# A four-layer transformer on one core: layer three's attention scores as full-array matmuls, and layer four's shared expert taken out of its attention

## The chip, the cores and the metric

One core of one Trainium2 chip runs the whole model in one launch. The metric is the device time in microseconds (us); lower is better. The kernel before takes 2572.56 us, the median of 3 runs (2572.2 to 2572.8).

## The reference

`x` is 16 sequences of 256 tokens, 128 wide, float32. Each of the four layers (0 to 3 in the code; "layer 2" below is the third, "layer 3" the fourth) computes `x + attention(LN(x)) + ffn(LN(x))`. What the change touches:

```python
# layer 2, attention: 16 heads of 8, causal
logits = einsum('bhsd,bhtd->bhst', q, k) / sqrt(8); masked; softmax; @ v; @ w_out
# layer 3, attention: 16 heads of 8, plus a 32-wide rotary part that all heads share
scores = einsum('bqhd,bkhd->bhqk', q, k) + einsum('bqr,bkr->bqk', q_rope, k_rope)[:, None]
scores = scores / sqrt(8 + 32); masked; softmax; @ v; @ W_o
# layer 3, ffn: 8 experts, each token to its best 2, and a shared expert for every token
out    = sum over the 2 chosen e: gate * (gelu(xf @ w1[e] + b1[e]) @ w2[e] + b2[e])
shared = gelu(xf @ ws1 + bs1) @ ws2 + bs2        # 128 -> 512 -> 128
return out + shared
```

## The kernel before

Tokens stand in 8 chunks of 512 (two sequences each). Every layer 1 to 3 runs five stages in this order, each closed for all engines before the next begins: R (normalise, turn, router logits), T (routing on VectorE, one step), A (attention), M (experts, on 256-slot tiles), C (combine: add the gated expert results to `x`). PE, ScalarE (ACT), VectorE (DVE), GpSimd (POOL) and SyncE (SP, which issues most DMAs) each have their own program in this order, tied by semaphores. `STAGES` (L76) gives each stage its count of steps, and `event(...)` (L395 on) how many times per step a semaphore is raised.

**Attention of layers 2 and 3** (`attention`, L951 for ACT, L1317 for PE, L2014 for DVE). A chunk has 16 steps; a step is one pair of heads of one sequence. In step p PE does, in this order: `scores(p)` (keys x queries, with minus the row maximum in an extra row, then the causal mask added by a 128-row matmul with the identity), `turn_maxima`, `average(p-1)` (18 matmuls of 9 columns), `maxima(p+LEAD)` (queries x keys, only to find the row maxima; again with masks), then `turn_o`, `out_proj` and a piece of the next chunk's projections (`prepare`). ACT reads each of the two score banks twice with Exp (`exps`, L1013). POOL makes the low half of the probabilities (`pair_low`, L763) and then, while any are left, sends one tile of 128 token rows to the experts' slots (`send_row_tile`, L744). DVE reduces the maxima (L2120, L2121). SP moves q and k rows through DRAM into stacks (`put_rows`, `load_heads`) and the maxima into the stacks' extra row (`send_rows`).

**The two layers' stacks.** In layer 2 a head stands on 32 rows of the stack: `rows_of` (L1387) returns rows 32j to 32j+32, so a score matmul contracts over 32 rows, and the two heads of a step lie on two different strips of the array. In layer 3 `rows_of` returns all 128 rows (96 rotary, 24 of the head's own, the maximum's row and blanks).

**The shared expert** is inside layer 3's attention: after `exps` of steps 9 to 12 ACT computes one quarter (128 of 512 hidden units) with Gelu (`shared`, L1022); PE computes the quarter's up product in the same steps (`shared_up`, L1478) and its down product one step later (`shared_down`, L1484), in float32; DVE adds the sum to `x` at step 14. Exp and Gelu are in different function tables.

**The router of layer 3** turns a chunk (4 transposes) and multiplies it by the router's weights (4 small matmuls) per chunk; the last combination (C3) has no work of PE or ACT. The outputs are sent after the last combination loads are issued (L709 to L711).

Of the kernel before, what the change touches and what calls it, by code (L numbers as in the profile page):

```python
# [22 lines left out]
ALU = mybir.AluOpType  # L23
ACT = mybir.ActivationFunctionType
# [6 lines left out]
P = 128  # L31
# [44 lines left out]
STAGES = {"N0": NCH, "L0": NCH}  # L76
# [66 lines left out]
def build_program(nc, A, out):  # L143
    ctx = ExitStack()
    with ctx:
# [21 lines left out]
        head_rows = nc.dram_tensor("head_rows", [2, HEADS, 4, 8, CHUNK], HALF).ap()  # L167
# [118 lines left out]
        shared_h = probT  # L286
        cT3 = oT[:, 1, :]
        q_stack = qT[:, 0:2, :].rearrange("p a c -> p (a c)").bitcast(HALF).rearrange("p (g c) -> p g c", g=4)
# [18 lines left out]
        def stack4(a):  # L307
# [5 lines left out]
        head_q = [stack4(far_stacks[:, 0:2048]), stack4(far_stacks[:, 4096:6144]), stack4(near_stacks[:, 0:2048]),  # L313
                  stack4(kT[:, :, :].rearrange("p a c -> p (a c)").bitcast(HALF))]
        head_k = [stack4(far_stacks[:, 2048:4096]), stack4(far_stacks[:, 6144:8192]), stack4(near_stacks[:, 2048:4096]),
                  stack4(region[:, 3072:4096].bitcast(HALF))]
# [10 lines left out]
        sco = [duo[:, 0, :], duo[:, 1, :]]  # L327

# [20 lines left out]
        blank_put = sem("blank_put")  # L349
# [45 lines left out]
        sh_up = event("sh_up", A3=FB)  # L395
        sh_act = event("sh_act", A3=FB)
        sh_down = event("sh_down", A3=FB)
        sh_added = event("sh_added", A3=1)
# [17 lines left out]
        c_step = event("c_step", C1=1, C3=1)  # L416

# [52 lines left out]
        HEAD0 = 96  # L470

# [49 lines left out]
        def _(sp):  # L521
# [53 lines left out]
            def feed_attention(layer):  # L575
# [7 lines left out]
                if layer == 2:  # L583
                    sp.wait_ge(stack_set, 1)
                    for kind in range(2):
                        sp.dma_start(head_rows[kind][:, 0, kind:8, :],
                                     k_stack[0:(8 - kind) * HEADS, 0, :]).then_inc(blank_put, 16)
                    sp.dma_start(head_rows[1][:, 0, 0, :], q_stack[0:HEADS, 0, :]).then_inc(blank_put, 16)
                    sp.wait_ge(blank_put, 48)

                def put_rows(n, kind):
# [5 lines left out]
                    for b, plane in enumerate(planes[kind]):  # L597
                        sp.dma_start(head_rows[kind][:, b + 1, :, :], parts[:, plane, :]).then_inc(rows_put[kind], 16)

                def load_heads(n, g, kind):  # L600
# [3 lines left out]
                    if layer == 3:  # L604
                        proj_read_v.wait(sp, stage, n, rope_made[kind])
                        sp.dma_start((head_q, head_k)[kind][g][0:HEAD0, :, :],
# [4 lines left out]
                    if layer == 2:  # L611
                        sp.dma_start((q_stack, k_stack)[kind][:, g, :], own.rearrange("j b e c -> (j b e) c"))\
                            .then_inc(stack_in[g], 16)
                    else:
                        sp.dma_start((head_q, head_k)[kind][g][HEAD0:P, :, :], own.rearrange("j b e c -> (b e) j c"))\
                            .then_inc(stack_in[g], 16)

                def send_rows(i, e):
# [4 lines left out]
                    dst = q_stack[0:P:GROUP, g, own] if layer == 2 else head_q[g][HEAD0:HEAD0 + 1, :, own]  # L623
                    sp.dma_start(dst, nm_rows[:, b, :]).then_inc(nm_in[b], 16)
# [192 lines left out]
        def _(act):  # L817
# [49 lines left out]

            def router(layer):
# [8 lines left out]
                with act.Fori(0, NCH - 1) as i:  # L877
                    turned_chunk(i + 1, False)
# [94 lines left out]
            def attention(layer):  # L973
# [48 lines left out]
                def shared(i, n):  # L1022
                    sh_up.wait(act, stage, i, n)
                    if n >= 2:
                        sh_down.wait(act, stage, i, n - 2)
# [1350 lines left out]
```

## Time and profile before

| | |
|---|---|
| median of 3 runs | 2572.56 us |
| the profiled execution's own time | 2563.02 us |
| its span (first to last instruction) | 2561.1 us |
| mean granted TensorE clock | 0.82 |
| PE busy, ACT busy, DVE busy, POOL busy | 1926.5, 1300.0, 1557.2, 1140.6 us |

Times of rows count from the span's start. PE is the matmul, PEld the weight load. "PEclk" is the granted TensorE clock, 1.00 being the higher of its two levels (2.4 GHz) and 0.50 the lower (1.2 GHz). A float32 matmul shows as two instructions. Layer 2's attention lies at about 1172 to 1616 us, layer 3's router and routing at 1776 to 1819, its attention at 1819 to 2345, its experts up to 2527, the last combination from there to the end.

### The profile page before, as it was taken

Reading aid. Unit: us, or ns where it says so; the run is one execution under the profiler, and the core shown is the slowest. Engines: PE = TensorE matmul, PEld = TensorE weight load, DVE = VectorE, ACT = ScalarE, POOL = GpSimd, SP = SyncE. Lnnn points to the kernel's source line nnn. Section 1 sums busy time; section 2 is a strip of 40 time slices with the busy share of each in tenths; the row PEclk is TensorE's granted clock in tenths of the full one; section 3 lists DMA queues with packets and bytes.
Section 4 is the critical chain, followed back from the end, with each engine's and each line's share of the span. In section 5 each row is a group of like instructions: output and inputs, shape, how many; then the busy total and the mean of one; then the engine's idle time right before and its main releaser. Section 6 shows DMA issues by size and latency. Waiting matters only on the chain.

```text
span 2561.1 us, 61860 instructions
## 1 busy us (share of the span) xinstructions
PE 1926.5 (75%) x21198; PEld 1285.9 (50%) x21199; DVE 1557.2 (61%) x3642; ACT 1300.0 (51%) x2667; POOL 1140.6 (45%) x921
## 2 busy tenths in 40 slices
PE   1553899899999688625999999682478877876993
PEld 0223566666666566522444444462255555554662
DVE  2236788787888788764444444576555555553775
ACT  0231577676777555302555555550166666665552
POOL 0003577674555233311764455342066664442552
PEclk9785899999999999955555565795689889997997
DMA  8900000020000111211211112121243333330224
GB/s 225 171 2 0 12 18 17 18 78 4 2 2 2 37 45 46 73 41 47 59 43 34 34 43 84 30 58 41 59 108 97 97 94 79 84 83 12 63 63 125
DMA packets 168827, 142.85 MB, mean 56 GB/s; under 512 B 16408, under 2 KB 155000, under 8 KB 168608
## 3 DMA queue, kind: packets, MB, share of 16 engines
q1 hardware_dynamic: 154944, 111.69, 17.9%
q0 software_dynamic: 11584, 23.91, 2.8%
q10 hardware_dynamic: 2080, 4.19, 0.5%
q8 instruction: 153, 2.51, 0.4%
q14 instruction: 66, 0.54, 0.1%
HBM read 62.04 MB, written 52.28 MB: 45 GB/s over the span
## 4 chain that ended last, share of the span: by engine, by line
PE 44%; DVE 19%; issue 12%; ACT 11%; POOL 9%; DMA 2%; DVEq 1%; SPq 1%; ACTq 0%; POOLq 0%
PE duo L1150 11%; PE mo L1150 8%; PE misc L1150 7%; PE ob L1150 7%; POOL v L765 6%; PE acc L1150 6%; ACT v L1020 3%; PE pt L1150 3%; ACT v L1019 2%; DVE nmax L2234 2%; DVE v L1933 2%; ACT L1019 2%; DVE region L2237 1%; ACT L1026 1%; DVE x L2003 1%
## 5 line engine op out<-in xcount | busy, mean ns | idle before, releaser
L765 POOL TENSOR_TENSOR v<-v 128x768 f16<-128x768 f32 x256 | 420.2, 1642 | 519.0 <-ACT v L1020 517.5
L760 POOL TENSOR_TENSOR v<-v 128x512 f16<-128x512 f32 x256 | 290.5, 1153 | 259.9 <-DVE region L2237 259.7
L787 POOL DMA_INDIRECT results<-probT,dest_no x202 | 218.2, 1080 | 325.4 <-ACT probT L819 285.2
L1150 PE MATMUL ob<-wm,v 128*128 128x9 f16 (+1 forms) x5856 | 258.2, 180 | 116.1 <-POOL v L765 94.6
L1150 PEld LDWEIGHTS ob<-wm,v 128*128 128x128 f16 x5856 | 216.7, 100 | 202.3 <-issue 95.0
L2120 DVE TENSOR_REDUCE nm<-duo 128x2 f16<-128x256 f32 x256 | 108.8, 425 | 332.1 <-PE duo L1150 332.1
L1019 ACT ACTIVATE v<-mo 128x384 f32<-128x384 f32 x352 | 174.2, 495 | 192.8 <-PE mo L1150 188.4
L1091 ACT ACTIVATE v<-mo 128x512 f32<-128x512 f32 x256 | 153.4, 599 | 161.1 <-PE mo L1150 161.1
L2234 DVE TENSOR_REDUCE nmax<-duo 128x2 f32<-128x512 f32 x256 | 164.9, 686 | 85.8 <-PE duo L1150 85.8
L1150 PE MATMUL duo<-kT,wm 128*128 128x256 f16 x1212 | 171.8, 279 | 54.7 <-DVE kT L1921 29.2
L1020 ACT ACTIVATE v<-mo 128x384 f16<-128x384 f32 x352 | 175.5, 499 | 0.0
L2121 DVE TENSOR_REDUCE nm<-duo 128x2 f16<-128x512 f32 x256 | 174.3, 681 | 0.0
L746 POOL DMA_INDIRECT slot_rows<-xd,slot_no x160 | 160.5, 1003 | 26.0 <-issue 25.7
L1150 PE MATMUL mo<-qT,kT 64*128 64x256 f16 (+2 forms) x1888 | 169.2, 286 | 0.0
L933 ACT ACTIVATE v<-duo,cols 128x256 f32<-128x256 f32 x248 | 104.1, 471 | 104.6 <-PE duo L1150 99.1
L1150 PEld LDWEIGHTS duo<-kT,wm 128*128 x1212 | 112.5, 99 | 81.3 <-issue 66.5
L1092 ACT ACTIVATE v<-mo 128x512 f16<-128x512 f32 x256 | 153.1, 598 | 0.0
L1925 DVE TENSOR_TENSOR v<-v 128x512 f16<-128x512 f32 x202 | 139.2, 689 | 4.4 <-ACT v L819 0.2
L1200 PE MATMUL pt<-ident,tmp 128*128 128x128 f32 x96 | 26.4, 431 | 143.7 <-DVE tmp L1777 139.1
L1150 PEld LDWEIGHTS mo<-qT,kT 64*128 64x128 f16 (+1 forms) x1888 | 81.3, 97 | 99.0 <-issue 87.8
L1150 PE MATMUL duo<-mask,ident 128*128 128x256 bf16 x512 | 130.4, 348 | 0.0
L1019 ACT ACTIVATE v<-pt 128x384 f32<-128x384 f32 x160 | 79.3, 496 | 84.2 <-PE pt L1150 82.3
(286 smaller groups left out, 4300.0 us busy)
## 6 DMA issues: line engine op xcount, KB each, us to landing
prob<-slot_rows SPq DMA_DIRECT2D x101, 130.0 KB, 2.2
head_rows<-v SPq DMA_DIRECT2D x96, 128.0 KB
load<-wm SPq DMA_DIRECT2D x32, 384.0 KB, 3.7
qT<-results SPq DMA_DIRECT2D x40, 256.0 KB, 3.1
qT<-head_rows SPq DMA_DIRECT2D x48, 128.0 KB, 2.1
qT<-wm SPq DMA_DIRECT2D x16, 384.0 KB
slot_rows<-prob SPq DMA_DIRECT2D x4, 1300.0 KB, 22.0
kT<-head_rows SPq DMA_DIRECT2D x40, 128.0 KB, 2.5
```

The costliest lines, as they stand in the source:

```text
L746: pool.indirect_dma_start(out=slot_rows[layer], out_offset=bass.IndirectOffsetOnAxis(ap=slot_no[:, j, t:t + 1], axis=0), in_=xd[:, t, :], ...
L760: pool.tensor_tensor(p16[:, p % 2, h, 1, :], p32[:, h, :], p16[:, p % 2, h, 0, :], ALU.subtract)\
L765: pool.tensor_tensor(p16_2[:, p % 2, 1, :], p32_2[:, p % 2, :], p16_2[:, p % 2, 0, :], ALU.subtract)\
L787: pool.indirect_dma_start(out=results[layer], out_offset=bass.IndirectOffsetOnAxis(ap=dest_no[:, 2 * b + t:2 * b + t + 1], axis=0), in_=y_ ...
L1019: act.activation(p32_2[:, p % 2, own], src, ACT.Exp)
L1020: act.activation(p16_2[:, p % 2, 0, own], src, ACT.Exp).then_inc(p_high.sem, 1)
L1091: act.activation(p32[:, h, :], mo[h][:, :], ACT.Exp)
L1092: act.activation(p16[:, p % 2, h, 0, :], mo[h][:, :], ACT.Exp).then_inc(p_high.sem, 1)
L1150: return pe.matmul(dst, lhsT, rhs, start=start, stop=stop)
L1925: dve.tensor_tensor(hb[:, h, 1, :], hid[:, h, :], hb[:, h, 0, :], ALU.subtract)\
L2121: dve.tensor_reduce(nm_own[:, e % 2, jj, 1, :], duo[:, :, P:LINE], AX.X, ALU.max, negate=True)\
L2234: dve.tensor_reduce(nmax[:, 2 * (p % 2) + h, :], sco[h][:, :].rearrange("p (q k) -> p q k", q=2), AX.X, ALU.max, negate=True).then_inc(nma ...
```

## The change

1. Layer 2's stacks: queries become one 96-row stack per head in which only the head's own 24 rows are filled and the others stay zero; the four heads of a group share one 96-row key stack, and the maximum has row 96. Score and maxima matmuls contract over 97 and 96 rows. The blank rows are no longer read through DRAM: DVE sets four query stacks (to 0) and rows 96 to 127 of the key stacks (to 1). A group's queries come by 4 DMAs instead of 1.
2. Layer 3: rows 96 to 127 of the key stacks are set to 1 by DVE at the attention's start.
3. The shared expert becomes a stage of its own, "S3": chunk 0 in the router R3, chunks 1 and 2 in T3, chunks 3 to 7 in the last combination C3. Its up products go to four PSUM banks.

```diff
-STAGES = {"N0": NCH, "L0": NCH}
+STAGES = {"N0": NCH, "L0": NCH, "S3": NCH}
-        head_rows = nc.dram_tensor("head_rows", [2, HEADS, 4, 8, CHUNK], HALF).ap()
+        head_rows = nc.dram_tensor("head_rows", [2, HEADS, 3, 8, CHUNK], HALF).ap()
-        shared_h = probT
+        shared_h = flat1[:, 0:4 * CHUNK].rearrange("p (n c) -> p n c", n=4)
+        shared_up_bank = [mo[0], mo[1], ob, sco[0]]
+        shared_out = [sco[1], acc]
-        SHARED_AT = {9: 0, 10: 1, 11: 2, 12: 3}
-        DOWN_AT = {10: 0, 11: 1, 12: 2, 13: 3}
+        EARLY = 3
-        REFILL = {2: 2, 3: 4}
+        REFILL = {2: 5, 3: 4}
# SP, load_heads
-                    if layer == 2:
-                        sp.dma_start((q_stack, k_stack)[kind][:, g, :], own.rearrange("j b e c -> (j b e) c"))\
+                    elif kind:
+                        sp.dma_start(k_stack[0:4 * OWN_ROWS, g, :], own.rearrange("j b e c -> (j b e) c"))\
                             .then_inc(stack_in[g], 16)
+                    else:
+                        for j in range(4):
+                            sp.dma_start(head_q[2][g][OWN_ROWS * j:OWN_ROWS * (j + 1), j, :],
+                                         own[j].rearrange("b e c -> (b e) c")).then_inc(stack_in[g], 16)
# SP, feed_attention: the three blank DMAs of layer 2 and the wait for them go; the loads are spread
-                next_at = {2: {6: both[0:2], 8: both[2:4], 12: both[4:6]},
+                next_at = {2: {6: both[0:2], 8: both[2:3], 9: both[3:4], 12: both[4:5], 13: both[5:6]},
-                last_at = {2: {0: both[6:8]}, 3: {0: both[6:7], 2: both[7:8]}}[layer]
+                last_at = {2: {0: both[6:7], 1: both[7:8]}, 3: {0: both[6:7], 2: both[7:8]}}[layer]
# PE, rows_of
-                    if layer == 2:
-                        r = head(g, jj, h)
-                        return q_stack[r, g, :], k_stack[r, g, :]
-                    return head_q[g][:, 2 * jj + h, :], head_k[g][:, 2 * jj + h, :]
+                    return head_q[layer][g][0:n, j, :], k_stack[0:n, g, :] if layer == 2 else head_k3[g][0:n, j, :]
# PE, router(3): shared_piece(i) behind logits(i), then around the ranks' matmuls
+                        if i < FB:
+                            shared_up(0, i)
+                        else:
+                            shared_down(0, i - FB)
...
+                    for n in range(FB):
+                        shared_up(1, n)
...          (here the ranks' two matmuls)
+                    for n in range(FB):
+                        shared_down(1, n)
+                        shared_up(2, n)
+                    for n in range(FB):
+                        shared_down(2, n)
+                    sh_added.wait(pe, "S3", EARLY - 1)
# PE, at the end
+            stage_closed(pe, "M3")
+            for n in range(FB):
+                shared_up(EARLY, n)
+            for c in range(EARLY, NCH):
+                for n in range(FB):
+                    shared_down(c, n)
+                    if c < NCH - 1:
+                        shared_up(c + 1, n)
# ACT: shared(0, i) behind turned_chunk(i + 1); shared(1, n) before the routing's Exp,
#      shared(2, n) before attention(3), shared(3..7, n) behind M3
-                        if layer == 3 and p in SHARED_AT:
-                            shared(i, SHARED_AT[p])
# DVE, router(3), ahead of ranks_full.wait
+                if layer == 3:
+                    add_shared(0)
# DVE, attention
-                    dve.memset(k_stack[:, 0, :], 0.0)
-                    dve.memset(q_stack[0:HEADS, 0, :], 1.0).then_inc(stack_set, 1)
+                    for a in head_q[2]:
+                        ins = dve.memset(a, 0.0)
+                    ins = dve.memset(k_stack[HEAD0:P, :, :], 1.0)
+                else:
+                    for a in head_k3:
+                        ins = dve.memset(a[HEAD0:P, :, :], 1.0)
+                ins.then_inc(stack_set, 1)
+                if layer == 3:
+                    for c in range(1, EARLY):
+                        add_shared(c)
+                    sh_added.wait(dve, "S3", EARLY - 1)
# DVE, combine(3): x_made of a chunk 3 to 7 is raised behind add_shared(c)
+                    if layer == 3 and c >= EARLY:
+                        last.then_inc(c_last, 1)
+                        dve.wait_ge(c_last, c - EARLY + 1)
+                        add_shared(c)
+                        sh_added.wait(dve, "S3", c)
+                        dve.sem_inc(x_made.sem, 1)
```

`add_shared(c)` waits for the chunk's last down product and adds `shared_out[c % 2]` to `x` with one 128x512 tensor_tensor. `head_q[2]`, `head_q[3]` and `head_k3` name the stacks' places (for layer 2 in `qT`, `region` and `prob`). The waits of layer 3's attention that belonged to the shared expert go with it.

## Rows read from the trace of the kernel before

**Rows 1.** The page's second part, the granted clock in 40 slices of 64 us.

```profile
PEclk9785899999999999955555565795689889997997
```

**Rows 2.** Busy time of each engine by stretch (us, instructions), then granted clock and DMA.

```profile
1302.00:1613.00 311.00, 282.20 (x3050) 135.09 (x3046) 139.63 (x321) 168.29 (x404) 156.75 (x97) 0.56 0.16 46
1776.00:1800.00 24.00, 19.92 (x96) 19.55 (x96) 17.62 (x64) 4.78 (x8) 0.28 (x1) 0.50 0.00 0
2106.00:2292.00 186.00, 148.28 (x1736) 106.49 (x1736) 95.35 (x202) 125.21 (x245) 80.94 (x50) 0.94 0.32 84
2292.00:2316.00 24.00, 18.05 (x291) 14.22 (x290) 12.97 (x33) 14.81 (x38) 14.94 (x10) 1.00 0.19 49
```

**Rows 3.** ACT in order of time: first Exp of steps 0, 10 and 16, a layer-2 chunk.

```profile
1356.48 0.49 ACT L1019 ACTIVATE v<-mo 128x384 f32<-128x384 f32 x1 [1.15 <-PE mo L1150]
1392.84 0.49 ACT L1019 ACTIVATE v<-pt 128x384 f32<-128x384 f32 x1 [2.33 <-PE pt L1150]
1410.37 0.49 ACT L1019 ACTIVATE v<-mo 128x384 f32<-128x384 f32 x1 [1.15 <-PE mo L1150]
```

**Rows 4.** PE, order of time: layer 2, then layer 3, both at the low clock.

```profile
1447.92 0.50 PE L1150 MATMUL duo<-kT,qT 32*128 32x128 f16 x4
1448.35 0.61 PE L1150 MATMUL duo<-mask,ident 128*128 128x256 bf16 x2
...
1839.88 0.82 PE L1150 MATMUL duo<-load 128*128 128x128 f16 x4 [7.87 <-DMA load<-head_rows]
1840.50 0.64 PE L1150 MATMUL duo<-mask,ident 128*128 128x256 bf16 x2
```

**Rows 5.** ACT, order of time: steps 9 and 16 of layer 3's sixth chunk; steps 4 and 8 of its last.

```profile
2202.72 0.48 ACT L1019 ACTIVATE v<-mo 128x384 f32<-128x384 f32 x1
2230.71 0.49 ACT L1019 ACTIVATE v<-mo 128x384 f32<-128x384 f32 x1 [0.59 <-PE mo L1150]
...
2302.30 0.49 ACT L1019 ACTIVATE v<-pt 128x384 f32<-128x384 f32 x1 [0.33 <-PE pt L1150]
2312.70 0.49 ACT L1019 ACTIVATE v<-mo 128x384 f32<-128x384 f32 x1 [0.20 <-PE mo L1150]
```

**Rows 6.** Groups by line in 2106 to 2292 us: busy us, mean ns, idle before.

```profile
L1026 ACT ACT_TABLE_LOAD x12 | 15.4, 1283 | 0.2
L1019 ACT ACT_TABLE_LOAD x12 | 15.4, 1283 | 0.2
L1026 ACT ACTIVATE probT<-misc,cols 128x512 f32<-128x512 f32 x12 | 8.3, 688 | 0.1
```

**Rows 7.** Groups by line, POOL, 1850 to 2106 us.

```profile
L765 POOL TENSOR_TENSOR v<-v 128x768 f16<-128x768 f32 x64 | 105.0, 1641 | 150.5 <-ACT v L1020 150.1
L746 POOL DMA_INDIRECT slot_rows<-xd,slot_no x63 | 64.5, 1024 | 10.3 <-issue 10.3
```

**Rows 8.** PE in order of time: float32 products of 512 columns, low clock, then high.

```profile
1820.54 2.04 PE L1150 MATMUL acc<-wm,region 128*128 128x512 f32 x2 [11.99 <-DVE wm L2023]
1822.38 1.68 PE L1150 MATMUL misc<-wm,region 128*128 128x512 f32 x2
...
1826.43 1.02 PE L1150 MATMUL acc<-oT,region 128*128 128x512 f32 x2
1827.37 1.13 PE L1150 MATMUL misc<-oT,region 128*128 128x512 f32 x2
```

**Rows 9.** DVE in order of time: the sets ahead of layer 2, and T3's ranks.

```profile
1171.81 0.27 DVE L2025 MEMSET kT<- 128x256 uint32 x1
1172.12 0.48 DVE L2026 MEMSET qT<- 16x512 f16 x1
...
1808.66 0.42 DVE L1860 COPY qT<-misc 128x256 f32<-128x256 f32 x1 [1.39 <-PE misc L1150]
```

**Rows 10.** All engines in order of time, the last combination.

```profile
2525.70 0.96 POOL L787 DMA_INDIRECT results<-probT,dest_no  x1 [0.30 <-issue]
2551.38 6.70 SPq L711 DMA_DIRECT2D out_dram<-x  x8
```

More of the change, by code:

```diff
@@ L582, in feed_attention @@
                 rope = kept[layer]["q"][0], kept[layer]["k"][0]
-                if layer == 2:
[L584 to L589, printed above, removed]
+                sp.wait_ge(stack_set, layer - 1)
                 def put_rows(n, kind):
@@ L866, in _, with shared @@
             copy(w1[:, 0, :], region[:, :]).then_inc(w1_high, 1)
+            def shared(c, n):
+                sh_up.wait(act, "S3", c, n)
+                if c:
+                    sh_down.wait(act, "S3", c - 1, n)
+                act.activation(shared_h[:, n, :], shared_up_bank[n][:, :], ACT.Gelu,
+                               bias=cols[:, ROW_BS1 + n:ROW_BS1 + n + 1]).then_inc(sh_act.sem, 1)
             def router(layer):
@@ L876, in router @@
                 turned_chunk(0, True)
-                with act.Fori(0, NCH - 1) as i:
-                    turned_chunk(i + 1, False)
+                if layer == 3:
+                    for i in range(NCH - 1):
+                        turned_chunk(i + 1, False)
+                        if i < FB:
+                            shared(0, i)
+                else:
+                    with act.Fori(0, NCH - 1) as i:
+                        turned_chunk(i + 1, False)
                 act.sem_inc(done["act"], 1)
+                if layer == 3:
+                    for n in range(FB):
+                        shared(1, n)
                 if layer == 2:
@@ L1020, in exps @@
                     act.activation(p16_2[:, p % 2, 0, own], src, ACT.Exp).then_inc(p_high.sem, 1)
[L1022 to L1025, printed above, removed]
-                    act.activation(shared_h[:, n % 2, :], misc[:, :], ACT.Gelu,
-                                   bias=cols[:, ROW_BS1 + n:ROW_BS1 + n + 1]).then_inc(sh_act.sem, 1)
                 def keep_o(i):
@@ L1188, in finish, with shared_up, shared_down @@
                 ins.then_inc(y_turned.sem, 1)
+            def shared_up(c, n):
+                if c:
+                    sh_act.wait(pe, "S3", c - 1, n)
+                mm(shared_up_bank[n][:, :], ws1[:, n * P:(n + 1) * P], turned_rows_of(3, c), True, True)\
+                    .then_inc(sh_up.sem, 1)
+            def shared_down(c, n):
+                dst = shared_out[c % 2]
+                if n == 0:
+                    if c >= 2:
+                        sh_added.wait(pe, "S3", c - 2)
+                    for t in range(TILES):
+                        mm(dst[:, P * t:P * (t + 1)], ones[0:1, :], bs2_row, t == 0, False)
+                sh_act.wait(pe, "S3", c, n)
+                for t in range(TILES):
+                    ins = mm(dst[:, P * t:P * (t + 1)], shared_h[:, n, P * t:P * (t + 1)], ws2[:, n, :], False,
+                             n == FB - 1 and t == TILES - 1)
+                ins.then_inc(sh_down.sem, 1)
             def router(layer):
@@ L2012, in step @@
                         measure(stage, c)
-                chunk_pairs(dve, step)
+                if layer == 3:
+                    for c in range(NCH):
+                        step(c, c // 2, c % 2, c < 2)
+                else:
+                    chunk_pairs(dve, step)
                 dve.sem_inc(done["dve"], 1)
@@ L2157, in chunk @@
                         if p == (8 if layer == 2 else 2) and begun:
-                            if layer == 3:
-                                sh_added.wait(dve, stage, i - 1)
                             add(acc_full, x_made, i - 1, 0)
-                        if p == 14 and layer == 3:
-                            add(sh_down, sh_added, i, FB - 1)
                         if more:
@@ L2166, in chunk @@
                         scale_o(i, 3)
-                        if layer == 3:
-                            sh_added.wait(dve, stage, i)
                         add(acc_full, x_made, i, 0)
```

105 lines of the change are left out of this document (52 added, 53 removed).

## The prediction

> **What bounds the kernel now.** I read the clock first: it is low in slices 19 to 25, which is layer 2's attention [rows 1]. Then the stretches. In 311 us of that attention PE is busy 282 us (91%) at a clock of 0.56, while ACT has 168, DVE 140 and POOL 157 us: the stage is bound by PE at its lower level. Layer 3's attention, the same loop with more to do, has 0.94, and its last chunk before the Gelus 1.00 [rows 2]. The chain of waits of the whole span (PE 44%, DVE 19%) averages over such stages and decides nothing here.
>
> The pace of a step comes from ACT's first Exp of each. Layer 2: steps 10 to 16 take 17.53 us, 2.92 a step; the chunk 53.9 us, so its first ten steps, with projections, 36.4 us [rows 3]. Layer 3's last chunk, between steps 4 and 8, no Gelu and the high clock: 10.40 us for four, 2.60 a step, maxima included. Layer 3's sixth chunk, steps 9 to 16: 27.99 us for seven; the other six chunks that have a successor lie between 27.7 and 28.7, and the last chunk's six intervals take 24.8 [rows 5]. In those seven intervals stand four Gelus, each with a table load of 1283 ns before it [rows 6] and another, as long, before the next Exp. A step with one needs four Exps (0.49 to 0.51 us), two loads and 0.69 us of Gelu on ACT, some 5 us: there ACT is the bound.
>
> **The change part by part.** The profiled execution took 2563.02 us, 1.9 over its span, and the median of the runs is 9.5 us above it. The sum is made against 2563.0 and 9.5 is added at the end.
>
> *Gelus out of layer 3's attention.* Removed from the path: steps 9 to 12 with their two loads each. What is late next: in the first four chunks POOL, which has its subtraction (1641 ns), a row send (1024 ns) and 0.16 us or more between them per step [rows 7], 2.9 us; in the next three the loop ACT, POOL, PE at the 2.60 of [rows 5]; in the last about 2.5. After: 4 x 7 x 2.9 + 3 x 7 x 2.6 + 6 x 2.5 = 81 + 55 + 15 = 151 us. Before: 7 x about 28.2 + 24.8 = 222 us. Gain 71, I take **-70**. Not less than -35 (the steps behind at 3.5 us, the pace that steps 0 to 5 have now with projections in them), not more than -85 (2.35 us a step, just above ACT's own four Exps). The rotary steps 3 to 8 stay: they wait for DVE, and nothing of theirs is removed.
>
> *Layer 2's matmuls over 96 and 97 rows.* Two effects. First, at one and the same low clock a group of four costs more, since the two heads no longer lie on two strips: from the first of the group to the mask behind it 0.43 us in layer 2, 0.62 us in layer 3, which has all 128 rows [rows 4]. Two groups a step, 128 steps: +0.38 x 128 = +49 us, if the clock stays. Second, the clock. Layer 3's steps of the same kind hold 1.00 for 24 us without projections and without the shared expert [rows 2], so the step with array-wide scores keeps it high; layer 2's, alike except for the 32 rows, are granted 0.56. I take 96 and 97 rows to stand nearer to 128 than to 32, and the clock to be high in most of the stage. A step then has 2.60 instead of 2.92 (POOL's 2.9 in the first two chunks, where rows are sent). The float32 work of a chunk (three projections, turn, output product, about 8 us low) halves, of which some 3.3 us show. Chunk: 16 x 2.6 + 3.3 = 45 us against 53.9 here and 53.2 in the mean of the five alike: -8 x 5; first two -3 each; last -3: -49 if always high. Clock dips as in layer 3 leave about two thirds: **-33**. Bounds: -55 and +49.
>
> SP's queue in layer 2: 34 issues a chunk instead of 22, at 0.4 to 0.65 us in SP's own rows in order of time: at most 22 of 46 us. The maxima's rows are sent behind them, but have four steps (10 us) before scores need them. Nothing on the path. Cost if that cover is gone: 2 us a chunk.
>
> *Entry to layer 2.* DVE's sets: zeros over 512 halves take 0.27 us, ones 0.48 [rows 9]; now four times 2048 zeros (1.07 each) and 2048 ones (1.94), 6.2 us instead of 0.75. DVE had 2 us to spare before the first low part, so 3.4 show; the three blank DMAs were hidden and give nothing. The first stack has three more issues, and six maxima are each 0.19 slower at the low clock. **+5**, bounds +2 and +8.
>
> *Chunk 0 in the router.* PE is already busy 19.9 of 24 us there at the low clock [rows 2]. A 512-column float32 product has 1.84 us from start to start low and 0.94 high [rows 8]; a down quarter (4 x 128 columns) as much. Seven pieces and one bias on the path: 8 x 1.8 = 14 us if low, near 0 if high, since DVE's normalising then hides them. **+8**, bounds 0 and +15.
>
> *T3.* Before the ranks: one down and four up pieces, 4.5 to 9 us, against 6.2 us of DVE's choice of experts; Exp waits behind four Gelus and a load. add_shared(0) fits into DVE's idle 1.39 us [rows 9]. **+2**, bounds 0 and +4.
>
> *Entry to layer 3.* Behind the ranks PE has 8 down and 4 up pieces and 2 biases, 13 us high, 24 low. DVE needs 10.2 us for the rest of T3 (from 1808.7 [rows 9] to its last instruction of the stage at 1818.9), then four sets of 2048 ones, 4 x 1.94 = 7.8 us by [rows 9], then two adds of 0.69; only then may PE project. It is DVE's line that ends last: **+9**, bounds +7 and +13.
>
> *Last combination.* Now 36 us, without PE. From the experts' close (about 2527 [rows 10]) PE does 5 x (4 up + 4 down + bias) = 45 pieces x 0.94 = 42 us high, 1.5 more until the clock rises. Then an add and an output DMA: outputs are now issued from 2551.4 to 2558.1 [rows 10] and the last has landed 3.0 us later; in the new order only the last chunk's is late, 0.5 us of issue and 3.0. 2527 + 43.5 + 0.7 + 3.5 = 2574.7 against 2561.1: **+13**, bounds +8 and +50 (all at the low level, 83 us of PE).
>
> *Sum:* -70 - 33 + 5 + 8 + 2 + 9 + 13 = **-66**. 2563.0 - 66 = 2497; plus 9.5: **2506.5 us**.
>
> **Rivals.**
> (a) *The clock stays low in layer 2.* Place: every group of scores and maxima in A2; price +49 instead of -33; it decides if 96 rows are granted no more than 32. Sum +16: 2588.6 us, slower than before. For it: PE is already busy 91% of that stage and yet is not granted more. Against: layer 3 falls to the low level too, at its start [rows 4], and is back at 0.94 and 1.00 in the same kind of steps [rows 2]. The Trainium skill, "TensorE: Matmul & The Clock Gate", section "Part 3: Packing small matmuls", speaks for this rival: matmuls with few contraction rows should be put on distinct strips, where they run at the same time. The trace agrees in the 0.43 against 0.62 us. By that rule alone the edit is a loss, and the sum would be this rival's.
> (b) *Layer 3 does not go at 2.6 to 2.9.* The stacks of the next chunk (384 KB each) have three steps from SP's issue until maxima need them: 15 us with Gelus, 8 without, for a load of about 5. If they or the contention with them set the pace, the gain is 35: 2541 us.
> (c) *The shared pieces run at the low level all the way.* +50 at the end, +15, +4, +13 before: sum -17, 2555 us. For it: R3 and T3 are at 0.50 now. Against: at layer 3's start the same kind of product stands first at 2.04 and 1.68 us, six microseconds later at 1.02 [rows 8].
> (d) *The clock is high throughout layer 2 and the router hides its pieces:* -49, 0, 0: sum -92, 2480 us.
> (e) *No difference:* terms cancel by chance, 2572.
>
> **How the numbers follow.** Forecast 2506.5 with 0.52; (a) 0.09, (b) 0.15, (c) 0.08, (d) 0.14, (e) 0.02. Range 2476 to 2553: it takes in (d), (b) and the better half of (c), and leaves out (a). A change of 0.2% (5 us) is about what can be told from none here. Faster: all but (a) and (e), less a little for mixtures of (a) with (b): 0.88; same 0.02; slower 0.10. The likeliest case's own range is 2490 to 2525.
>
> **What would show it.** PEclk of layer 2's attention at 0.85 or more, its steps at 2.6 to 2.9, the stage 20 to 45 us shorter; a group of four at 0.32 us. Layer 3's attention: three or four table loads of ACT in the whole stretch from R3 on instead of 64, chunks of 52 to 56 us instead of 61 to 65. PE in the last combination some 40 us without a gap, the stage 12 to 15 us longer. First maxima of layer 3 about 9 us later behind the ranks. The prediction is wrong if the clock of layer 2 stays under 0.7, if layer 3's steps 9 to 15 take over 3.2 us each, or if the last combination passes 60 us.

## The result and the profile after

The changed kernel takes 2510.89 us (median of 4 runs, 2509.32 to 2516.36) against 2572.38 us of the kernel before on the same chip (4 runs): ratio 0.9769, interval 0.9755 to 0.9783. Forecast was 2506.5, range 2476 to 2553. The profiled execution took 2516.36 us with a span of 2514.2: 46.9 us less span than before, while the medians differ by 61.5. The profiled run of before lies 9.4 us under its median, that of after 5.5 above its own, and that is the gap between the two figures.

The page after, PE's line of the first part and the clock of the second; slices are now 63 us ([rows 1] are the same line of before, the 5s of slices 19 to 25 were layer 2's attention):

```profile
PE 1907.0 (76%) x21198; PEld 1363.1 (54%) x21199; DVE 1575.3 (63%) x3649; ACT 1221.9 (49%) x2607; POOL 1139.9 (45%) x921
PEclk9785799999999899955677776696777878988999
```

Busy time by stretch of the kernel after, columns as in [rows 2]: layer 2's attention from first to last Exp; router 3; T3; the 24 us behind T3, in which the entry to layer 3's attention begins; layer 3's attention with the last 17 us of its entry (its first Exp stands at 1851.8); the first 40 us of PE's work for the last combination:

```profile
1200.00:1596.00 396.00, 343.99 (x4055) 247.59 (x4054) 185.47 (x428) 223.07 (x538) 238.50 (x159) 0.70 0.17 47
...
1762.80:1792.20 29.40, 25.79 (x137) 21.34 (x138) 17.62 (x64) 8.70 (x13) 0.00 (x0) 0.67 0.00 1
1792.20:1810.70 18.50, 16.68 (x93) 11.60 (x93) 15.96 (x51) 8.30 (x11) 0.00 (x0) 1.00 0.01 1
1810.70:1834.70 24.00, 12.04 (x41) 5.96 (x39) 15.29 (x21) 2.39 (x4) 0.00 (x0) 0.79 0.11 29
...
1835.00:2284.00 449.00, 343.43 (x4170) 243.87 (x4170) 250.39 (x514) 227.48 (x545) 273.68 (x191) 0.84 0.35 94
...
2467.00:2507.00 40.00, 39.74 (x209) 27.10 (x210) 19.65 (x64) 13.75 (x20) 1.92 (x2) 0.96 0.52 152
```

Layer 2's clock rose from 0.56 to 0.70 only. In the last combination PE works without a gap from 2467.3 to 2510.6, 43.4 us, where 43.5 was worked out. Stage by stage, between the same marks in both profiled executions (us). A body goes from the first Exp to the last step's Exps; an entry begins at the end of DVE's last routing instruction and ends in layer 2 with the first Exp, in layer 3 with DVE's first reduction of maxima; a router, T3 and the last combination begin with DVE's first instruction:

| | before | after | forecast | measured |
|---|---|---|---|---|
| entry to layer 2's attention | 27.6 | 32.5 | +5 | +4.9 |
| its body | 415.5 | 396.7 | -33 | -18.8 |
| router 3 | 23.8 | 29.5 | +8 | +5.7 |
| T3 | 18.6 | 18.4 | +2 | -0.2 |
| entry to layer 3's attention | 22.3 | 32.2 | +9 | +9.9 |
| its body | 490.7 | 432.1 | -70 | -58.6 |
| last combination | 29.1 | 39.7 | +13 | +10.6 |
| layer 2's experts; layers 0 and 1 | | | 0 | +3.0; -3.0 |

The rest (layer 3's experts) is -0.4; the sum is -46.9.

**Steps of the two attentions.** "The interval behind step n" is from the first Exp of step n to that of the next step. ACT of the kernel after in order of time, first Exp of a step: layer 2, steps 10 and 16 of the third chunk, at the low clock; layer 3, steps 9, 10 and 16 of the sixth chunk (answers to [rows 3] and [rows 5]):

```profile
1333.65 0.49 ACT L1039 ACTIVATE v<-pt 128x384 f32<-128x384 f32 x1 [2.55 <-PE pt L1167]
...
1351.80 0.49 ACT L1039 ACTIVATE v<-mo 128x384 f32<-128x384 f32 x1 [1.24 <-PE mo L1167]
...
2171.20 0.49 ACT L1039 ACTIVATE v<-mo 128x384 f32<-128x384 f32 x1
...
2172.70 0.52 ACT L1039 ACTIVATE v<-pt 128x384 f32<-128x384 f32 x1
...
2189.59 0.49 ACT L1039 ACTIVATE v<-mo 128x384 f32<-128x384 f32 x1 [0.60 <-PE mo L1167]
```

Layer 3's seven intervals take 18.39 us, where [rows 5] had 27.99; with the other chunks 20.7, 20.0, 20.6, 20.0, 17.4, 18.4, and 14.7 in the last: 150 us in all, where 151 was forecast. So the part that was to bring 71 us brought 72. Layer 2's six intervals (1333.65 to 1351.80) take 18.15 us, 3.03 a step at the low clock, against 2.92 before: +0.1, where +0.38 was taken.

**What layer 3 gave back.** After step 8 it did not go as before. DVE of the kernel after in order of time, behind step 8 of the second chunk: the sum of the rotated keys, a cast, the subtraction for their low part, and the copy of the maxima for which PE waits:

```profile
1937.84 1.15 DVE L2123 TENSOR_TENSOR prob<-prob 128x512 f32<-128x512 f32 x1
1939.02 0.42 DVE L2125 CAST wm<-prob 96x512 f16<-96x512 f32 x1
1939.48 2.59 DVE L2128 TENSOR_TENSOR wm<-prob,wm 32x512 f16<-32x512 f32 x1
1942.11 0.41 DVE L2174 CAST xnT<-duo 4x256 f16<-4x256 f32 x1
```

POOL and PE of the same kernel beside it:

```profile
1939.87 1.65 POOL L768 TENSOR_TENSOR v<-v 128x768 f16<-128x768 f32 x1
...
1942.66 0.59 PE L1167 MATMUL duo<-region,kT 120*128 120x128 f16 x3 [3.56 <-DVE xnT L2174]
```

The same place and chunk of the kernel before, DVE and then POOL:

```profile
1944.69 0.69 DVE L2063 TENSOR_TENSOR prob<-prob 128x512 f32<-128x512 f32 x1
1945.42 0.45 DVE L2065 CAST wm<-prob 96x512 f16<-96x512 f32 x1
1945.90 0.68 DVE L2068 TENSOR_TENSOR wm<-prob,wm 32x512 f16<-32x512 f32 x1
1946.62 0.41 DVE L2114 CAST xnT<-duo 4x256 f16<-4x256 f32 x1
...
1946.13 1.95 POOL L765 TENSOR_TENSOR v<-v 128x768 f16<-128x768 f32 x1 [0.49 <-ACT v L1020]
```

A subtraction on 32 rows takes 0.68 us. Where POOL's subtraction (1.64 us alone) overlaps it behind step 8, one of the two gets longer ("pays" below): DVE's takes 2.0 to 2.6, or POOL's 1.8 to 2.2. They overlap there in all seven chunks that have a successor. Before, DVE paid 3 times (the interval behind step 8 is then 8 to 9 us instead of 4.9 to 5.1), after, 6 times. The seven intervals sum to 46.0 before and 56.8 after: 10.8 us given back, and with them -72 becomes about -61. Steps 0 to 5 of the chunks are 2.6 us longer in sum, which makes the table's -58.6; why is not shown. The Trainium skill, "SBUF — State Buffer", section "SBUF: two separate sides", has the rule: a DVE operation with two SBUF inputs and a GpSimd one take a shared pair of ports in turn, the loser blocked for the whole instruction. The rows agree in that behind step 8 the two never both kept their length; that the one which starts first wins they don't show, since DVE began 0.39 us ahead of POOL (1939.48 and 1939.87) and paid.

### The profile page after: what moved, and what is told of

Same layout as the page of the kernel before. It is cut to its first block, busy times and chain, and to the rows that moved or that the text cites. A ratio compares the mean times of both kernels' runs of the same rounds, so it can differ in the third digit from the quotient of the medians.

```text
span 2514.2 us, 61783 instructions
## 1 busy us (share of the span) xinstructions
PE 1907.0 (76%) x21198; PEld 1363.1 (54%) x21199; DVE 1575.3 (63%) x3649; ACT 1221.9 (49%) x2607; POOL 1139.9 (45%) x921
## 4 chain that ended last, share of the span: by engine, by line
PE 47%; DVE 20%; issue 11%; POOL 11%; ACT 8%; DMA 2%; DVEq 1%; SPq 1%; ACTq 0%; POOLq 0%
PE duo L1167 12%; PE mo L1167 9%; POOL v L768 7%; PE ob L1167 7%; PE misc L1167 7%; PE acc L1167 6%; PE pt L1167 3%; ACT v L1040 3%; DVE nmax L2288 2%; ACT v L1039 2%; DVE v L1973 2%; DVE region L2291 1%; DVE v L1965 1%; POOL rstd L736 1%; DVE stats L1795 1%
## 5 line engine op out<-in xcount | busy, mean ns | idle before, releaser
L1167 PE MATMUL mo<-qT,kT 64*128 64x256 f16 (+2 forms) x1712 | 144.9, 276 | 0.0
L1167 PEld LDWEIGHTS mo<-qT,kT 64*128 64x128 f16 (+1 forms) x1712 | 86.6, 98 | 74.0 <-issue 60.2
```

The lines of the kernel that those rows point to most:

```text
L1167: return pe.matmul(dst, lhsT, rhs, start=start, stop=stop)
```

## The experiments

Theory A: the terms of the prediction, each in its own place, and the clock of layer 2 is held back because products over 96 rows still leave the fourth strip of 32 rows idle. The rival: the clock is held back by too little work and not by unfilled rows, and layer 3's giving back comes from the stacks' loads or the clock and not from DVE and POOL. Ratios are against the kernel before, run beside them: e1 to e4 on one chip (before 2570.06 us), e5 to e8 on a second (2572.07), e9 to e11 on a third (2592.27). Each expectation was written before its run, but with the result above known.

**Each part alone.** e1: parts 1 and 2 of the change on the kernel before; e2: part 3 on the kernel before.

```diff
# e1: layer 2's array-wide stacks, DVE's sets, SP's four DMAs; the shared expert stays in layer 3's attention
-                    if layer == 2:
-                        r = head(g, jj, h)
-                        return q_stack[r, g, :], k_stack[r, g, :]
+                    return head_q[layer][g][0:n, j, :], k_stack[0:n, g, :] if layer == 2 else head_k3[g][0:n, j, :]
# e2: the new stage S3; layer 2's stacks as before
-STAGES = {"N0": NCH, "L0": NCH}
+STAGES = {"N0": NCH, "L0": NCH, "S3": NCH}
```

> Only the first edit: layer 2's stacks of 96 and 97 rows (and the ones set in layer 3), the shared expert stays in layer 3's attention. Theory: its gain is the granted clock of layer 2's attention alone: the clock there rises from 0.56 to about 0.73, the stage is 19 us shorter, its entry 5 us longer, 2 to 8 us more for the ones set ahead of layer 3: 2555 to 2566 us against 2572. Rival 1 (the rows do nothing, all gain comes from the Gelus): clock 0.56, time 2575 or more. Rival 2 (the gain needs both edits, since they shift each other's phases): layer 3's attention changes by more than 8 us too.

> Only the second edit: the shared expert beside the router and the last combination, layer 2 as before. Theory: layer 3's attention 55 to 70 us shorter, router +6, entry to layer 3 only +2 (no ones to set, the two adds remain, but PE's twelve pieces end about 22 us behind the ranks instead of 11, so perhaps +9 as well, if PE's line and not DVE's sets it), last combination +11: 2522 to 2532 us. Rival (collisions of DVE's 32-row subtraction with POOL's subtraction give gain back): at least 5 of the 7 chunks have an interval of 8 to 9 us behind step 8, as in the changed kernel (6 of 7) and unlike the kernel before (3 of 7).

Measured: e1 2568.86, ratio 1.0001 (0.9982 to 1.002); e2 2521.41, ratio 0.9821 (0.9784 to 0.9859). Both attentions of e1, layer 2's first, then of e2, busy time by stretch (e2's second stretch begins 17 us ahead of its first Exp):

```profile
1205.00:1597.00 392.00, 338.14 (x4054) 243.53 (x4052) 185.50 (x427) 222.98 (x539) 239.10 (x159) 0.71 0.17 47
1841.00:2344.00 503.00, 402.41 (x4534) 287.44 (x4535) 248.13 (x510) 330.78 (x641) 274.36 (x191) 0.88 0.30 80
```

```profile
1197.00:1612.00 415.00, 377.41 (x4054) 178.60 (x4052) 186.46 (x427) 224.21 (x537) 238.28 (x159) 0.55 0.17 49
1841.00:2289.00 448.00, 336.42 (x4170) 241.27 (x4170) 249.87 (x513) 227.24 (x544) 273.38 (x191) 0.87 0.37 98
```

The gain in time is the shared expert's. Layer 2's stacks make their own stage 23 us shorter in e1, but the two entries take 5 more each and layer 3's body 12 more (502.6 against 490.7), with 6 long subtractions where the profiled run of before has 3. In layer 3's attention e1 changes only the blank rows (they are set by DVE, and the products contract over 120 and 121 rows instead of 128): it starts at another time, and DVE and POOL meet otherwise. So e1's forecast gain of 6 to 17 us did not come, and its rival 2 did (layer 3 changed by more than 8 us). e2 lies 0.6 us under its forecast range; its layer 3 body is as short as after's, and 6 of its 7 chunks have the long interval (8.2 to 9.1 us), as its rival said: taking the shared expert out is enough for that. Its entry to layer 3, with the adds but without the sets, is no longer than before (30.2 against 30.6 us from DVE's first instruction of the stage to the first Exp); e1's, with the sets but without the adds, is 5.0 longer, and with both it is 9.9. The two parts do not add up in time either: 0 and 46 us in the ratios' terms, 59 together.

**More rows in layer 2.** e3 puts the maximum's row of layer 2 at 120, where layer 3 has it: maxima contract over 120 rows, scores over 121; the rows between are zero in the queries. e8 is the same on e1's kernel, with the shared expert inside the attention.

```diff
-        MAX_ROW = {2: 4 * OWN_ROWS, 3: HEAD0 + OWN_ROWS}
+        MAX_ROW = {2: HEAD0 + OWN_ROWS, 3: HEAD0 + OWN_ROWS}
```

> The changed kernel with layer 2's maximum in row 120 instead of 96 (rows 97 to 119 zero in the queries): scores contract over 121 rows, maxima over 120 instead of 96, so that both reach into all four strips of 32 rows. Theory (the clock that is granted rises with the rows in use): clock of layer 2's attention from 0.73 to over 0.80, the stage 5 to 15 us shorter. Rival (rows beyond the first strips do not matter; what holds it low is how seldom PE streams): clock 0.71 to 0.75, time 2508 to 2513 us, the same as the changed kernel.

> Layer 2's stacks with rows 120/121 and the ones set, the shared expert still in layer 3's attention. Theory: layer 2's attention is bound by the granted clock alone, so it takes 373 us here as well at a clock of 0.85, against 415 before and 392 with rows 96/97; the sets cost 5 us at each entry: 2542 to 2552 us. Rival (the clock of layer 2 rose because of something in the other edit): 385 us or more for that stage, 2560 us or more.

Measured: e3 2489.39, ratio 0.9686 (0.9649 to 0.9723), 21.5 us under the kernel after; e8 2536.42, ratio 0.9864 (0.9842 to 0.9886). Both gain somewhat more than their theories said, and both rivals are out. Layer 2's body in e3, then in e8:

```profile
1204.00:1577.00 373.00, 297.36 (x4054) 220.00 (x4052) 184.62 (x427) 222.89 (x539) 239.85 (x159) 0.85 0.18 50
```

```profile
1203.00:1569.00 366.00, 290.31 (x4054) 215.41 (x4052) 184.61 (x427) 222.03 (x539) 239.15 (x159) 0.87 0.18 50
```

Same number of matmuls, same columns, 24 more rows: the clock goes from 0.70 to 0.85 and the stage from 396.7 to 373.3 us. In e8 the stage is 48.7 under that of before, which is the best bound that the prediction set (-49). Of e3's 21.5 us some 4 are not the rows': router 3 falls from 29.5 to 25.3 us, at a granted clock of 0.79 instead of 0.67, but in e5 and e6, with the same rows and nothing edited in the router, it takes 31.2 at 0.63.

Whether it is the number of rows that counts, or that the maxima's products now reach the fourth strip, no run separates: nothing between 96 and 120 rows was run.

**More work at 96 rows.** e4 gives PE of the kernel after one superfluous maxima matmul (256 columns, 96 rows) per step of layer 2.

```diff
+                    if layer == 2:
+                        q, k = rows_of(g, jj, 0, MAX_ROW[layer])
+                        mm(duo[:, 0, P:LINE], q[:, q0 + P:q0 + SEQ], k[:, k0:k0 + SEQ], True, True)
```

> The changed kernel with one more matmul a step in layer 2: a 256-column maxima product done twice, the first result overwritten, 128 times. Its own price is about 0.11 us at the high and 0.21 us at the low clock, so 14 to 27 us if the clock stays as it is: 2524 to 2538 us. Theory (layer 2 is short of granted clock): the clock rises to 0.85 or more and pays for it, 2495 to 2512 us. Rival (PE's work itself is the bound whatever the clock): slower by 14 us or more.

Measured: 2514.41, ratio 0.9788 (0.9753 to 0.9822), within the intervals the same as after. The stretch of layer 2's body in e4:

```profile
1206.00:1599.00 393.00, 342.12 (x4177) 250.60 (x4176) 186.02 (x428) 222.40 (x539) 239.04 (x159) 0.75 0.17 47
```

128 more matmuls make PE no busier (342 us against 344) since the clock rises from 0.70 to 0.75 and the stage takes 393.4 us against 396.7: the added work pays for itself and no more. Neither side of the expectation holds: the clock did not come to 0.85, and the time did not grow by 14 us. The theory that too little work holds the clock back is right in part; filled rows are the better means.

**The collision taken away.** e5 is e3 with the keys' 32-row subtraction moved from the end of step 7's DVE work to the start of step 8's `prepare`, behind the copy of the maxima; e6 moves the queries' one, with the low part of the keys behind it, from step 5 to 6 in the same way.

```diff
                         if p == 7:
-                            rotated_parts(i, 9, after["k"][0], ((32, 64),))
+                            rotated_parts(i, 9, after["k"][0], ((32, 64),), 0)
                         if p == 8:
+                            rotated_parts(i, 9, after["k"][0], ((32, 64),), 1)
# e6 as well: rotated_parts(i, 3, ...) part 0 in step 5, part 1 in step 6
```

> The kernel with rows 120/121 (2489 us) and one DVE instruction of layer 3's attention moved: the 32-row subtraction that ends the keys' rotation goes from the end of step 7 behind the maxima of step 8. Theory: that subtraction lasts 2.0 to 2.6 us instead of 0.68 when POOL's subtraction runs beside it, and at its old place the copy of the maxima, and so PE, wait behind it: the intervals behind step 8 fall from 8 to 9 us to 4 to 6, six or seven of them, 15 to 28 us off the whole: 2461 to 2474 us. Rival (PE waits there for the chain of projections and DVE's work as a whole, wherever the long instruction stands): the intervals move to step 9 or stay, time 2484 to 2494 us.

> As the run with the keys' subtraction moved, and the queries' one (with the low part of the keys behind it) moved from step 5 to step 6 as well. Theory: the interval behind step 6, 4.7 to 6.4 us now, falls by 1 to 2 us in each chunk: 8 to 15 us less than the run with one moved. Rival (its copy of maxima is not late there, and the later low part delays PE's fourth rotary product and the rows' DMA): the same or up to 10 us more than with one moved.

Measured: e5 2465.81, ratio 0.9582 (0.9563 to 0.9601); e6 2450.32, ratio 0.9535 (0.9512 to 0.9559). DVE of e5 in order of time, the same place of the second chunk:

```profile
1909.61 0.44 DVE L2131 CAST wm<-prob 96x512 f16<-96x512 f32 x1
1909.98 0.40 DVE L2183 CAST xnT<-duo 4x256 f16<-4x256 f32 x1
...
1912.33 0.68 DVE L2125 TENSOR_TENSOR wm<-prob,wm 32x512 f16<-32x512 f32 x1
```

Layer 3's attention in e6, from 16 us ahead of its first Exp:

```profile
1808.00:2217.00 409.00, 334.87 (x4170) 234.22 (x4170) 236.24 (x513) 226.51 (x545) 273.78 (x191) 0.87 0.39 103
```

In e5 the copy now follows the cast, no subtraction of the 16 is over 0.70 us, and the interval behind step 8 is 4.0 to 4.6 in all seven chunks. The seven sum to 29.8 us against 56.1 in e3, 26.3 less. Layer 3's body falls by 19.3 us (431.4 to 412.1), in part because the steps from step 9 on take 5.4 longer and the clock is 0.83 where e3 has 0.86: the clock did not bring the gain. The medians differ by 23.6. That is inside the theory's range, and the rival is out.

e6's move shortens the interval behind step 6 from 4.8 to 6.2 us to 3.3 to 3.5, 16.1 us in the seven; layer 3's body falls to 392.7 and the median by 15.5. This is not the collision with POOL. The subtraction that was moved takes 0.68 us in every chunk of before, after and e5. DVE of e5 in order of time, the second chunk, and then the same place in e6:

```profile
1900.36 0.42 DVE L2131 CAST wm<-prob 96x512 f16<-96x512 f32 x1
1900.81 0.68 DVE L2136 TENSOR_TENSOR wm<-prob,wm 32x512 f16<-32x512 f32 x1
1901.53 0.69 DVE L2105 SCALAR_TENSOR_TENSOR v<-acc,v 128x512 f16<-128x512 f32 x1
1902.13 0.40 DVE L2183 CAST xnT<-duo 4x256 f16<-4x256 f32 x1
```

```profile
1896.95 0.42 DVE L2131 CAST wm<-prob 96x512 f16<-96x512 f32 x1
1897.29 0.41 DVE L2184 CAST xnT<-duo 4x256 f16<-4x256 f32 x1
```

Here two DVE instructions of ordinary length stood ahead of the copy that PE waits for, 1.4 us, and they went behind it. Why the interval varies between 4.7 and 6.4 us in the kernels without this move is not shown.

**The same moves on the kernel before** (e10), and **the table loads of before alone** (e11: the shared expert's Gelu is replaced by Identity, which leaves its function out; the 64 loads go, PE's products stay).

```diff
# e10: e6's moves of the two subtractions, on the kernel before
# e11:
-                    act.activation(shared_h[:, n % 2, :], misc[:, :], ACT.Gelu,
+                    act.activation(shared_h[:, n % 2, :], misc[:, :], ACT.Identity,
```

> The kernel before, with only the two subtractions of the rotations moved a step later; Gelus and 32-row stacks as they were. Theory (the collision with POOL was in the kernel before as well, in some chunks of some runs, and makes its runs spread over 2557 to 2576): intervals behind step 6 at 3.3 to 3.5 us, behind step 8 at 4 to 5, layer 3's attention 20 to 35 us shorter, 2538 to 2552 us, and its runs spread less. Rival (with Gelus on ACT the stall is made up in the steps behind it): 2560 us or more.

> The kernel before with the shared expert's Gelu replaced by Identity, which needs no other table: the 64 table loads go, and the 32 ACT instructions, all float32 products and their waits stay in layer 3's attention. The Gelu itself is left out. Theory (the table loads are what the Gelus cost): steps 9 to 12 at 2.9 to 3.3 us instead of 4.95, layer 3's attention 45 to 60 us shorter, almost as much as by moving the whole expert, 2512 to 2530 us. Rival (PE's float32 products and their waits bound those steps too): steps 9 to 12 at 3.8 us or more, 2540 us or more.

Measured: e10 2554.63, ratio 0.9841 (0.982 to 0.9863); e11 2554.54, ratio 0.9847 (0.983 to 0.9863). They ran on another chip, on which the kernel before takes 2592.27 us (by the traces of e10 and e11 against before's, each experts' stage of layer 2 and 3 takes 7 to 10 us longer there, what stands ahead of layer 2's attention 5 to 7, and layer 2's attention the same). ACT of e11 in order of time, step 10 of the sixth chunk:

```profile
2208.55 0.48 ACT L1019 ACTIVATE v<-pt 128x384 f32<-128x384 f32 x1
...
2211.32 0.69 ACT L1026 ACTIVATE probT<-misc,cols 128x512 f32<-128x512 f32 x1 [1.15 <-PE misc L1150]
2213.93 0.49 ACT L1019 ACTIVATE v<-mo 128x384 f32<-128x384 f32 x1 [1.92 <-PE mo L1150]
```

The kernel before, where the loads stand, end of step 9 of that chunk (its first Exp is in [rows 5]):

```profile
2204.37 1.28 ACT L1026 ACT_TABLE_LOAD   x1
2205.67 0.69 ACT L1026 ACTIVATE probT<-misc,cols 128x512 f32<-128x512 f32 x1
2206.37 1.28 ACT L1019 ACT_TABLE_LOAD   x1
2207.67 0.49 ACT L1019 ACTIVATE v<-pt 128x384 f32<-128x384 f32 x1
```

e10: layer 3's body is 462.9 us, 28 under before's, with no long subtraction: 16.2 us less behind step 8, 14.4 less behind step 6. The median is 37.6 under before's, where 20 to 34 were expected; the rival is out. But its runs spread over 13.4 us (2546.5 to 2559.9), those of before beside them over 7.3: the expectation that they spread less missed, so something else than these collisions spreads them too.

e11: 464.8, although DVE pays in 7 subtractions. Its seven intervals behind step 9 take 22.7 to 24.2 where before has 27.7 to 28.7, and with the last chunk's the loads are worth 39 us of the 72. The intervals behind step 8 take 14 of them back, so the body is 26 us under before's, not 45 to 60 as the theory had it, and steps 9 to 12 take 3.8 us in the mean, as the rival had it; the time, 37.7 us under before's, lies between the two. In what is left ACT waits for PE at each quarter (5.38 us from 2208.55 to 2213.93). The other 33 us are PE's float32 products, the 0.69 us on ACT and the round that they make; no run separates these. The Trainium skill, "ScalarE: Activation LUTs", section "What ACT_TABLE_LOAD costs", puts a switch at 2.66 us, half of it a drain behind the load. The rows of before show 1.28 and the next instruction 0.02 later, and 4.95 us from Exp to Exp; no drain stands there.

**The entries and the end.** e7 is e3 with the blank rows of the keys set as float32 words (two ones in each), and with PE and ACT entering the last combination without waiting for POOL. e9 is e6 and e7 together.

```diff
-                        ins = dve.memset(a[HEAD0:P, :, :], 1.0)
+                        ins = dve.memset(a[HEAD0:P, :, :].rearrange("p j c -> p (j c)").bitcast(F32), TWO_ONES)
-            stage_closed(pe, "M3")
+            stage_nearly_closed(pe, "M3")
+            y_made.wait(pe, "M3", SLOT_TILES[3] - 1)
```

> The kernel with rows 120/121 and two edits at stage boundaries: the ones are written two at a time as float32 words of the same bits (half the elements), and PE and ACT begin the last combination without waiting for POOL's last sends of the experts. Theory: sets of 2048 ones fall from 1.8 to 1.9 us to about 1.0, so 3.5 us at layer 3's entry and up to 1 at layer 2's; the last combination's PE work begins 3 us earlier and ends so: 2489 - 7 = 2480 to 2484 us. Rival (at either end something else is ready no sooner: PE's pieces for chunks 1 and 2, or the result loads): 2486 to 2490 us.

> Rows 120/121, both subtractions of the rotations moved a step later, the ones as float32 words, the last combination not waiting for POOL. Theory: the edits are at different places and add: 2450 less 3 us, 2444 to 2450. Rival: the phases they shift bring the collisions back at another step: over 2455.

Measured: e7 2486.41, ratio 0.9666 (0.965 to 0.9683); e9 2460.21 on the other chip, ratio 0.9491 (0.9462 to 0.9521), the best ratio of all. One of the four sets in the kernel after, then in e7 (DVE in order of time):

```profile
1812.69 1.76 DVE L2081 MEMSET load<- 32x2048 f16 x1 [0.48 <-issue]
```

```profile
1789.35 0.91 DVE L2089 MEMSET load<- 32x1024 f32 x1 [0.27 <-issue]
```

The entry to layer 3 falls by 3.6 us (31.9 to 28.3) and that to layer 2 by 1.1, as the theory said of the sets. The last combination falls by 1.3 instead of 3, and counted from layer 3's last Exp to the end only 0.4 is left. The medians of e3 and e7 differ by 3.0, inside their spreads, and the time lies in the rival's range. e9's expectation was in the second chip's terms; on the third, where before takes 20 us more, only its ratio can be held against e6's. It has no long subtraction and intervals of 4.2 to 4.3 us behind step 8, so the collisions did not come back.

## Why the prediction was right, and where it was off

The mechanism of the largest term stands: ACT was the bound in steps 9 to 12 of layer 3, and with the shared expert away the steps from 9 on go at 2.5 to 3.0 us. The time is 4.4 us over the forecast, inside its narrow range, but that closeness is luck in good part. Between the profiled executions the terms sum to -66 and the measured stages to -46.9, 19 us less. The forecast added 9.5 us because the profiled run of before lay so far under its median; that of after lay 5.5 above its own, and these 15 us hid most of the miss. Some of the signs named in advance came (four table loads from router 3 to the end of layer 3's attention, the first maxima 9.9 us later, PE without a gap at the end), others did not: the clock of layer 2 at 0.85, its stage 20 us or more shorter, all chunks of layer 3 at 52 to 56 us (they take 51 to 60). By its steps:

- *Gelus out of layer 3's attention*, -70: the part from step 9 on gave 72. The step that failed is "The rotary steps 3 to 8 stay: they wait for DVE, and nothing of theirs is removed." Nothing was removed, but they came to lie otherwise beside POOL, and three more of DVE's subtractions paid: 10.8 us back. The intervals behind step 8 in the profile of before (5 or 9 us) had shown that two lengths existed for one piece of work. In every profile a long interval there goes with a long subtraction of DVE, and e5 takes both away; e6 shows that those steps held another 16 us of DVE's order which has nothing to do with POOL.
- *Layer 2's rows*, -33: mis-sized, -18.8, by "the clock to be high in most of the stage". It was 0.70: 96 and 97 rows came out halfway between 32 (0.56) and 120 (0.85), not nearer to the full array as was taken. e3 (0.85) against the kernel after (0.70) shows that the rows move the clock with everything else the same; e4 (0.75) shows that they are not the only thing that does. The prediction called itself wrong under 0.7: it stands on that edge. The other half of the term was too pessimistic: +0.38 us a step at the low clock was +0.1. PE of both kernels at the low clock, from the average's matmuls through the maxima and their mask to the scores, after and then before:

```profile
1340.21 0.64 PE L1167 MATMUL ob<-wm,v 128*128 128x9 f16 x18
1340.70 0.80 PE L1167 MATMUL duo<-kT,qT 96*128 96x128 f16 x4
1341.30 0.63 PE L1167 MATMUL duo<-mask,ident 128*128 128x256 bf16 x2
1341.72 0.42 PE L1167 MATMUL pt<-prob,kT 97*128 97x256 f16 x1
```

```profile
1396.24 0.64 PE L1150 MATMUL ob<-wm,v 128*128 128x9 f16 x18 [0.20 <-POOL v L765]
1396.82 0.50 PE L1150 MATMUL duo<-kT,qT 32*128 32x128 f16 x4
1397.25 0.61 PE L1150 MATMUL duo<-mask,ident 128*128 128x256 bf16 x2
1397.79 0.50 PE L1150 MATMUL mo<-qT,kT 32*128 32x256 f16 x4
```

  The group itself goes from 0.43 to 0.60 us, as [rows 4] said. But in the kernel before, the average ahead of it has 0.58 us instead of 0.49, and the mask behind it 0.54 instead of 0.42: from the first line to the last 1.55 us before, 1.51 after. That is no single case: over the steps of layer 2 at the low clock the medians are 0.57, 0.43, 0.54 before and 0.50, 0.59, 0.43 after. The work on strips cost its neighbours what it saved itself. The price was read from the group alone and not from what stood around it; rival (a), which rests on that price and on the Trainium skill's advice to put small matmuls on distinct strips ("TensorE: Matmul & The Clock Gate", section "Part 3: Packing small matmuls"), would have been about +13 and not +49 even at the low clock (an estimate: 0.1 us in 128 steps).
- *Entries* +5 and +9: +4.9 and +9.9. A set of ones takes 1.76 and one of zeros 0.91 (1.94 and 1.07 taken), and the adds behind them are the last thing before PE's first product in layer 3.
- *Router and T3*, +8 and +2: +5.7 and -0.2. PE is busy 25.8 of 29.4 us at a clock of 0.67, between the two levels, as the middle value supposed; behind it the clock is 1.00 through T3, so its pieces hid entirely. The +5.7 is one draw: in the eight profiles of kernels that have these pieces in the router it takes 25.3 to 31.5 us, against 23.8 without them.
- *Last combination*, +13: +10.6. 45 pieces in 43.4 us at 0.96, one output DMA late.
- Rival (b) is out: steps go at 2.5 to 3.0 with the same stacks. (c) is out by 0.96 at the end (its own sum is -16, not -17). (d) did not come, though e8 shows that its -49 in layer 2 was to be had with 24 more rows.

The spans differ by 46.9, the medians by 61.5. One possible reason is the number of collisions that a run of before loses (e10 gains 37.6 us in the medians and 28 in its layer 3 body), but only profiled runs show that number, and e10's runs, with none in the profile, spread by 13.4 us all the same: it stays open.

The lowest time is e6's, 2450.32 us with 2572.07 for the kernel before on its chip; the kernel after has 2510.89 against 2572.38. e9 adds the ends' edits and has the lowest ratio, but the two intervals overlap.

## What to carry to other kernels

Where one piece of work has two lengths in one profile (5 and 9 us behind the same step), find what decides between them before pricing an edit elsewhere: a shift in time can turn it, and here that gave back 11 us of a term of 70 and took half of what layer 2's new stacks gained by themselves. Keep a DVE operation with two SBUF inputs away from the place where PE waits for DVE, if POOL streams beside it; and put what PE waits for ahead of the DVE work that can wait, collision or not (e6). And price a matmul's shape from the start of the work before it to the start of the work behind it, with the clock that its rows are granted.

## What was not expected of the hardware

- The granted clock of one stage: 0.56 with 32 rows in the products of scores and maxima, on strips, 0.70 with 96, and with the same matmuls and columns 0.85 to 0.87 with 120. Superfluous work may cost nothing: 128 matmuls more, the stage not longer (e4).
- Four matmuls on strips cost the full-array work around them about 0.1 us on either side at the low clock (0.57 against 0.50 us ahead of them, 0.54 against 0.43 behind).
- A DVE subtraction of 0.68 us takes 2.0 to 2.6 beside POOL's, or POOL's 1.64 takes up to 2.19, though the program ties the two together by no semaphore there.
- Two function-table loads and a Gelu between Exps cost their own 1.28, 0.69 and 1.28 us and nothing more (4.95 us from Exp to Exp, the rest is four Exps).
